# Edge table: both one-hots of a pair in one VectorE operation, stored interleaved

## The reference, cut to what matters

```python
edge_index = jnp.stack([src, dst])
h = jnp.maximum(_layernorm(x, axis=-1), 0.0)
x = x + _L0_gnn_ref(h, edge_index, L0_gnn_W1, ...)       # GCN, three aggregations
h = jnp.maximum(_layernorm(x, axis=-1), 0.0)
x = x + _L1_gnn_ref(h, edge_index, ...)                  # segment_sum of relu messages
h = jnp.maximum(_layernorm(x, axis=-1), 0.0)
x = x + _L2_gnn_ref(h, src, dst)                         # degree-normalised sum
h = jnp.maximum(_layernorm(x, axis=-1), 0.0)
x = x + _L3_gnn_ref(h, edge_attr_16, ...)                # attention over the edges of a node

# in each of the first three layers, in some form:
msg = norm[:, None] * h[row]
agg = jax.ops.segment_sum(msg, col, num_segments=N)
```

## Time and profile before

| | |
|---|---|
| median of three runs | 2812.8 us |
| profiled execution | 2815.78 us, span 2813.8 us |
| mean granted clock of TensorE | 0.827 of full speed |
| edge table (`fill_edges`) | about 122 to 510 us of the span |
| busy over the whole span | PE 80%, DVE 80%, ACT 61%, POOL 49% |

### The profile page before, as it was taken

One profiled execution on the slowest core, in us unless ns is written; L12 is line 12 of the kernel. 1 busy time (PEld: TensorE's weight loads), 2 busy tenths in 40 slices (PEclk: granted clock), 3 DMA queues, 4 the chain that ended last, 5 costly groups with the idle time before them and its releaser, 6 DMA issues. The chain is left out here.

```text
span 2813.8 us, 36452 instructions
## 1 busy us (share of the span) xinstructions
PE 2243.2 (80%) x7875; PEld 973.6 (35%) x7876; DVE 2252.1 (80%) x3833; ACT 1720.9 (61%) x6801; POOL 1375.4 (49%) x1141
## 2 busy tenths in 40 slices
PE   1488888897759988478898898989998989988850
PEld 0144444454425543222333333333333333333220
DVE  7699999413437761179999999999999999999966
ACT  3277777201101112088888888888888888888823
POOL 6100000004654000377777777777777777777403
PEclk9599999887779999668778778788888888888875
DMA  2000000003668542112222222222222222222213
GB/s 57 17 0 0 0 0 0 2 1 121 196 214 255 163 148 90 21 34 71 71 72 83 76 71 75 71 71 71 71 71 71 79 71 71 71 71 71 72 63 99
DMA packets 119351, 206.15 MB, mean 73 GB/s; under 512 B 54149, under 2 KB 75798, under 8 KB 113438
## 3 DMA queue, kind: packets, MB, share of 16 engines
q1 hardware_dynamic: 77294, 156.28, 16.1%
q0 software_dynamic: 41904, 48.40, 7.7%
HBM read 76.22 MB, written 128.39 MB: 73 GB/s over the span
## 5 line engine op out<-in xcount | busy, mean ns | idle before, releaser
L1753 POOL DMA_INDIRECT hs<-h_table,gix x880 | 1133.8, 1288 | 391.6 <-issue 294.3
L1846 ACT ACTIVATE e<-wps,hs 128x32 f32<-128x32 f32 x5632 | 1017.1, 442 | 176.1 <-PE wps L1777 142.0
L1777 PE MATMUL wps<-w_edge,ef 18*128 18x512 f32 x1760 | 629.4, 794 | 207.2 <-DVE e L1883 105.6
L1799 PE MATMUL slot_sums<-e,ident 128*128 128x512 f32 x1408 | 744.4, 678 | 9.4 <-DVE e L1948 7.0
L1799 PEld LDWEIGHTS slot_sums<-e,ident 128*128 128x128 f32 x1408 | 288.3, 216 | 485.8 <-issue 444.6
L1777 PEld LDWEIGHTS wps<-w_edge,ef 18*128 18x128 f32 x1760 | 176.6, 224 | 615.3 <-ACT e L1846 258.6
L517 ACT CAST edges<-acc 128x400 f32 x600 | 295.2, 492 | 121.0 <-PE acc L504 94.8
L542 POOL DMA_INDIRECT got<-in_edge_rows,start x64 | 71.1, 1112 | 587.4 <-POOLq L785 568.2
L500 PE MATMUL acc<-q_hot,lo_hot 128*128 128x400 bf16 x1200 | 307.2, 338 | 54.3 <-DVE q_hot L474 52.0
L1883 DVE TENSOR_TENSOR e<-wps,hs 128x2048 f32<-128x2048 f32 x132 | 301.9, 2287 | 23.1 <-PE wps L1777 22.1
L474 DVE TENSOR_SCALAR q_hot<-qcol,qT 128x400 bf16<-128x400 bf16 x1200 | 290.6, 319 | 1.0 <-PE acc L504 0.8
(11 more groups left out here) (374 smaller groups left out, 1963.9 us busy)
## 6 DMA issues: line engine op xcount, KB each, us to landing
rows_state<-states SPq DMA_DIRECT2D x44, 1280.0 KB, 4.8
rows_shift<-shifts SPq DMA_DIRECT2D x44, 640.0 KB, 3.0
got_order<-edges_order SPq DMA_DIRECT2D x56, 256.0 KB, 3.3
ef_order<-efT SPq DMA_DIRECT2D x56, 256.0 KB, 3.4
hs<-h_table,gix POOLq DMA_INDIRECT x880
ef<-ef_order SPq DMA_DIRECT2D x44, 320.0 KB, 3.0
edges_order<-got POOLq DMA_DIRECT2D x32, 256.0 KB, 2.5
edges_order<-msg_parts POOLq DMA_DIRECT2D x24, 256.0 KB, 3.5
```

What stands on the lines that cost most here:

```text
L1753: nc.gpsimd.indirect_dma_start(out=hs[u][:, s, :], out_offset=None, in_=d["h_table"], in_offset=bass.IndirectOffsetOnAxis(ap=gix[u][:, s:s ...
L1777: nc.tensor.matmul(wps[:, bank, :], ef[u][k:k + KM, g * P:(g + 1) * P], w[k:k + KM, :], start=True, stop=True).then_inc(a_mult, 1)
L1799: ins = nc.tensor.matmul(sums[:, g % 2, :], ident[:, :], e[u][:, g * SLOTS + c, :], start=(c == 0), stop=(c == SLOTS - 1))
L1846: ins = nc.scalar.mul(e[u][:, s, at], wps[:, bank, at], hs[u][:, s, f:f + 1])
```

## The change

`q_hot` and `qcol` get the two halves as the innermost dimension, and `qT` becomes bf16 with the halves side by side, as `loT` already is. One comparison of two tensors then makes the 800 values of a pair: `qcol` with each column number twice, against the pair's two values of `qT`, repeated over the 400 columns. The matmul of half s reads every second element of `q_hot`. The waits, the semaphores and the numbers of buffers stay as they are.

```diff
-        "qT": sb("qT", [P, 2, PAIR_TILES * P]),
+        "qT": sb("qT", [P, PAIR_TILES * P, 2], BF16),
         "lane": sb("lane", [P, P, 2 * HOTS], BF16),
-        "qcol": sb("qcol", [P, QW], BF16),
+        "qcol": sb("qcol", [P, QW, 2], BF16),
...
-                v.add(nc.vector.tensor_copy(qcol[:, :], qcolI[:, :]))
+                v.add(nc.vector.tensor_copy(qcol[:, :, :], bc(qcolI[:, :], 2, 2)))
...
-                    v.add(nc.vector.tensor_copy(qT[:, :, k * P:(k + 1) * P], tr[:, k, 0:2, :]))
+                    v.add(nc.vector.tensor_copy(qT[:, k * P:(k + 1) * P, :].rearrange("p n s -> p s n"), tr[:, k, 0:2, :]))
...
-        q_hot = sb("q_hot", [P, HOTS, 2, QW], BF16)
+        q_hot = sb("q_hot", [P, HOTS, QW, 2], BF16)
...
-                        for s in range(2):
-                            at = bass.ds(i * BODY + k, 1)
-                            ins = nc.vector.tensor_scalar(q_hot[:, k % HOTS, s, :], qcol[:, :], qT[:, s, at], None,
-                                                          ALU.is_equal)
-                        ins.then_inc(hot, 1)
+                        both = qT[:, bass.ds(i * BODY + k, 1), :].rearrange("p n s -> p (n s)")
+                        nc.vector.tensor_tensor(q_hot[:, k % HOTS, :, :], qcol[:, :, :], bc(both, 1, QW), ALU.is_equal
+                                                ).then_inc(hot, 1)
...
-                            nc.tensor.matmul(total, lo_hot[:, k // HOTS % 2, :, k % HOTS * 2 + s], q_hot[:, k % HOTS, s, :],
+                            nc.tensor.matmul(total, lo_hot[:, k // HOTS % 2, :, k % HOTS * 2 + s], q_hot[:, k % HOTS, :, s],
                                              start=(s == 0), stop=False)
```

## The result

The changed kernel has a median of 2819.59 us over 11 runs (2817.73 to 2825.19), the kernel before 2813.97 us over 11 (2811.42 to 2818.04). The ratio is 1.0018, with a 95% interval of 1.0009 to 1.0026: 5 us slower, between 2.5 and 7.3. The profiled execution spans 2817.8 us.

A forecast was written before the change was run, and what follows sets the result against it. Per 20 pairs, VectorE alone bounds two five-pair groups and a chain through TensorE's pause the other two. 190 ns plus 19 ns make 0.21 us, x 30 = 6.3 us more, so 2819.1 us; range 2811 to 2830.

The forecast's parts named there:

- the bound of 5.6 us: Whole program: a change under 0.2% (5.6 us) cannot be told from none; slower was given 0.66, same 0.29.
- The pair operation's price: VectorE's two-tensor comparison of 800 elements: 571 ns long, one every 485 ns, 19 ns more a pair than before.
- Rival B: VectorE's pair operation runs at the f32 slope, 899 ns: +244 us, 3057 us in all; chance 0.07.
- Two groups by VectorE, two by TensorE's chain: Every 20 pairs, two five-pair groups pay VectorE's extra 190 ns; the two around TensorE's pause mostly hide theirs.
- The 19 ns a stretch for the later one-hots: Chain around TensorE's pause: a pair's one-hots ready after 571 instead of 552 ns, 19 ns once per 20 pairs.
- TensorE's spread read at nothing: One-hot matmuls reading every second column, four bytes apart: still one every 169 ns, no cost.
- The forecast's own sign of being wrong, a step above 169 ns: One-hot matmuls on TensorE: starts more than 169 ns apart would show that the spread columns cost.
- rival A: TensorE's spread columns cost up to 1.46 times, so TensorE binds throughout: +65 us, 2878 us; chance 0.09.
- a tenth more on each matmul: TensorE's one-hot matmuls: 17 ns on two matmuls would lengthen the five-pair chain 0.17 us per 20 pairs, 5 us in all.
- the bound of 1.46: Upper limit for TensorE's spread read, from weight loads: 140 ns at 20 bytes apart against 96 packed.
- Rival C: VectorE's pair operation comes every 443 ns, the scalar one-hot having 24 ns fixed: -8 us, 2805 us; chance 0.07.
- Setup: Ahead of the loop: writing qcol at most 0.35 us more, copies to qT hidden; nothing, or up to 2.5 us uncovered.

The follow-up runs named there:

- r2: The changed kernel with qT left in f32, so one input of the pair operation is f32; ratio 1.0855 against the kernel before.
- n1: The kernel before, with TensorE and ScalarE reading the strip numbers once ahead of the loop, so without TensorE's pause; ratio 0.9941 against the kernel before.
- n2: The changed kernel, with TensorE and ScalarE reading the strip numbers once ahead of the loop, so without TensorE's pause; ratio 0.9983 against the kernel before.
- e2: The changed kernel, but TensorE reads 400 packed columns of the interleaved one-hot; ratio 1.0010 against the kernel before, stage +6.0 us.
- e1: The kernel before with its scalar one-hots written packed, but TensorE reads every second column; ratio 1.0009 against the kernel before, stage +1.7 us.
- r1: The kernel before, but the one-hot matmuls read columns 2, 4, 8, 16 and 20 bytes apart from a tile of zeros; one profiled run, 3115.8 us.
- r3: The changed kernel, but the pair operation compares all 800 values with one scalar; ratio 0.9976 against the kernel before.
- e3: The kernel before with eight instead of five one-hot buffers and the waits set accordingly; ratio 0.9964 against the kernel before.

## Why the prediction was right

The forecast was 6.3 us more; measured are 5 (2.5 to 7.3) by the ratio and 6.4 in the stage, 6.9 when the 13 turns stand for all. The median is 2819.6 us, the forecast one 2819.1. By its size the loss lies across the bound of 5.6 us that was drawn between slower and the same.

- **The pair operation's price:** 571 ns long and a step of 485 were forecast from L470 and the f32 rows; 565 and 486 measured, and the groups bound by VectorE grew from 3.07 to 3.16 us, the 95 ns forecast. Inner rows of two cost nothing more, and the Trainium skill's dearer lone words (Vector Engine (DVE) Microarchitecture Reference, 5.2) do not show for one word read again. Rival B is refuted for bf16, and r2 shows that its price was right for f32 (+244 forecast, +241 in the stage).
- **Two groups by VectorE, two by TensorE's chain:** confirmed by n1 and n2 (11 us apart without the pause, 11.4 forecast for it) and by the waits: 0.61 us became 0.47, where 0.17 less was forecast. The 19 ns a stretch for the later one-hots in this chain came out at some 10 in e2, where the read is packed; too small to matter.
- **TensorE's spread read at nothing:** the step that was off, by little. It costs 13 ns a matmul (182 against 169) and about 1 us in the stage, by e1 and by e2. The forecast's own sign of being wrong, a step above 169 ns, did appear, without the price of rival A. It had also reckoned that a tenth more on each matmul would lengthen the chain by 0.17 us a stretch, 5 us in all. By the same working 13 ns would be 0.13 us a stretch, 3.9 us; measured is a quarter of it. The reason, as far as the traces tell, is a wait that the forecast did not reckon with: the pair's 0.54 us hang on the third matmul and ScalarE's copy and not on the two one-hot matmuls.
- **Where luck helped:** the bound of 1.46 was read from weight loads; r1 shows that moving columns at their distance of 20 bytes take four times as long, so the bound was far too low for that distance, and it was the short distance that saved the forecast. Rival A would need 232 ns a matmul, which lies between r1's 0.18 us at 4 bytes and its 0.35 at 8.
- **The Trainium skill's 16-byte lines** (SBUF — State Buffer, section on the DMA port swizzle): two accesses in one line should give the full rate. At 4 bytes, with four in a line, the cost is some 8% (182 against 169 ns), and at 8 bytes, with two in a line, r1 measures twice the time. For TensorE's moving columns the measurement decides against that rule.
- **Rival C:** refuted, as the step is 486 ns and not 443. Its assumption was that the scalar one-hot streams at 0.52 ns an element. r3 measures 0.26, so the fixed part of the scalar one is 129 ns, not 24.
- **Setup:** L368 takes 557 instead of 350 ns, and the wait of L371 behind it falls from 1.2 to 1.0 us, so it was hidden, as said:

```profile
L371 DVE TENSOR_SCALAR_CACHE_REDUCE below<-cuts,pair 128x403 bf16<-128x403 f32 x5 | 3.2, 640 | 1.1 <-PE cuts L315 1.0
...
L368 DVE CAST qcol<-qcolI 128x800 bf16<-128x800 int32 x1 | 0.6, 557 | 0.0
```

## What to carry to other kernels

Before merging two operations into one of twice the length, find the rate of both kinds: here a scalar comparison streamed bf16 at twice the rate of a two-tensor one, so the time saved by one instruction less was lost again to slower elements. Look next at which engine each stretch of the loop really waits for: a pause of another engine hid part of a loss here, and could hide part of a gain just as well. And the cheap gain stood beside the change: three more buffers took 10 us off the kernel before, because they let VectorE work on through TensorE's pause (its waits for TensorE before L470 fell from 11.6 to 4.6 us in all).

## What the hardware showed that I had not expected

TensorE's moving bf16 columns, 400 of them at granted clock 1.00, took 0.17 us from one start to the next when packed, about 0.18 at a distance of 4 bytes, 0.35 at 8, 0.70 at 16 and 0.70 at 20 (r1). Weight loads at 20 bytes apart took 140 ns against 96 packed, so the two reads do not scale alike. The kernel before took 2883 us on one chip and 2814 on another; by the trace of e3 on the slower one, what follows the edge table took 67 us more there, nearly all of the difference.
